# Gate product and residual addition of batches 1 to 5: from VectorE to ScalarE copies and GpSimd products

## The reference

```
xz = rmsnorm(xn) @ in_proj.T;  x_s, z = halves of xz          # 256 channels each
u  = silu(conv4(x_s) + bias)
dt, B, C = u @ x_proj.T;  delta = softplus(dt @ dt_proj.T + b)
h[t] = exp(delta[t] * A) * h[t-1] + delta[t] * u[t] * B[t]    # 16 states per channel
y[t] = sum over states of h[t] * C[t]  +  u[t] * D
mamba = (y * silu(z)) @ out_proj.T + xn
out = x + mamba + (top-2-of-8 experts: silu(xn Wg) * (xn Wu) @ Wd)
```

## Time and profile before

| | |
|---|---|
| median of 3 runs | 635.2 us (634.61 to 636.0) |
| profiled execution, its own time | 637.19 us |
| its span, first to last instruction | 635.4 us |
| VectorE busy | 600.0 us, 94% |
| TensorE busy | 548.8 us, 86% |
| GpSimd busy | 490.9 us, 77% |
| ScalarE busy | 443.7 us, 70% |

### The profile page before, as it was taken

How to read it: one execution, slowest core, us unless ns; L and a number is a source line. 1 busy time by engine, 2 the same in 40 slices (tenths; PEclk the granted TensorE clock), 3 DMA queues, 4 the chain that set the end, 5 groups by cost and what they waited for, 6 DMA issues and landing times.

```text
span 635.4 us, 11450 instructions
## 1 busy us (share of the span) xinstructions
PE 548.8 (86%) x3560; PEld 428.1 (67%) x3560; DVE 600.0 (94%) x867; ACT 443.7 (70%) x891; POOL 490.9 (77%) x466
## 2 busy tenths in 40 slices
PE   5969988898899988989889898998989797878887
PEld 2368666655777777777688677776777465656564
DVE  6966989999999999999999999999999999899997
ACT  1784899128676787667766686776876479969881
POOL 5795039639989799897989879897897877875783
PEclk9867979979999999999999999999999989899999
DMA  7420107924667897777778796678884346332473
GB/s 222 145 84 0 63 10 124 316 101 158 208 230 271 261 304 261 251 254 250 264 263 267 240 300 242 235 262 273 292 269 149 124 162 217 128 118 77 113 146 87
DMA packets 60893, 122.99 MB, mean 194 GB/s; under 512 B 8218, under 2 KB 41378, under 8 KB 53794
## 3 DMA queue, kind: packets, MB, share of 16 engines
q1 hardware_dynamic: 53826, 112.42, 52.0%
q0 software_dynamic: 6288, 9.52, 6.7%
q10 hardware_dynamic: 720, 0.33, 0.2%
HBM read 112.77 MB, written 9.47 MB: 192 GB/s over the span
## 4 chain that ended last, share of the span: by engine, by line
PE 37%; DVE 27%; issue 14%; ACT 12%; POOL 10%; DMA 1%; DVEq 0%; POOLq 0%; ACTq 0%
DVE bank L1091 11%; DVE h_sb L1108 7%; POOL dbu L895 6%; PE bank L1522 6%; PE bank L1375 6%; PE bank L1407 5%; PE bank L1536 4%; PE bank L1530 3%; ACT dbu L530 3%; PE bank L1430 2%; ACT da L502 2%; PE bank L1422 2%; PE bank L1338 2%; POOL xs L882 1%; PE bank L1503 1%
## 5 line engine op out<-in xcount | busy, mean ns | idle before, releaser
L895 POOL TENSOR_TENSOR dbu<-du,xn_all 128x512 f32<-128x512 f32 x172 | 215.4, 1275 | 48.0 <-DVE bank L1091 47.5
L1091 DVE TENSOR_TENSOR_SCAN bank<-bank,dbu 128x512 f32<-128x512 f32 x170 | 207.7, 1224 | 3.4 <-ACT bank L514 3.4
L514 ACT ACTIVATE bank<-delta,a_sb 128x512 f32<-128x512 f32 x170 | 117.0, 690 | 76.9 <-DVE h_sb L1108 76.3
L1108 DVE TENSOR_TENSOR h_sb<-bank,xh_all 128x512 f32<-128x512 f32 x240 | 159.9, 680 | 1.2
L1375 PE MATMUL bank<-id_sb,h_sb 128*128 128x128 f32 x992 | 135.1, 281 | 15.3 <-DVE h_sb L1108 13.7
L1375 PEld LDWEIGHTS bank<-id_sb,h_sb 128*128 128x128 f32 x992 | 115.4, 145 | 27.1 <-DVE h_sb L1108 20.6
L1091 DVE TENSOR_TENSOR_SCAN bank<-da,bank 128x512 f32<-128x512 f32 x82 | 96.8, 1216 | 17.0 <-PE bank L1338 16.9
L1522 PEld LDWEIGHTS bank<-wd_sb,hid 117*128 117x128 f32 (+1 forms) x432 | 55.1, 190 | 55.0 <-DVE hid L1142 31.3
L1522 PE MATMUL bank<-wd_sb,hid 117*128 117x128 f32 (+1 forms) x432 | 64.0, 284 | 25.1 <-ACT xT L667 13.0
L882 POOL DMA_INDIRECT xs<-xn_rows,src x72 | 70.7, 981 | 12.1 <-issue 6.3
L530 ACT ACTIVATE dbu<-du_t,bc_sb 128x256 f32<-128x256 f32 x164 | 69.4, 496 | 4.3 <-DVE bank L1091 2.9
(11 more groups left out here) (192 smaller groups left out, 877.9 us busy)
## 6 DMA issues: line engine op xcount, KB each, us to landing
xh_all<-b_rows SPq DMA_DIRECT2D x30, 1024.0 KB, 6.4
xn_all<-b_rows SPq DMA_DIRECT2D x25, 1024.0 KB
wgu_sb<-in_w_gu SPq DMA_DIRECT2D x72, 352.0 KB, 4.4
wd_sb<-in_w_dn SPq DMA_DIRECT2D x72, 192.0 KB, 5.5
y_slots<-ys SPq DMA_DIRECT2D x72, 64.0 KB
xn_rows<-xn_all SPq DMA_DIRECT2D x2, 1040.0 KB, 11.8
out<-x_sb SPq DMA_DIRECT2D x7, 256.0 KB, 7.5
x_sb<-in_x SPq DMA_DIRECT2D x2, 640.0 KB, 6.3
```

Source lines behind the costliest of these rows:

```text
L514: nc.scalar.activation(bank_of(b, m)[:, :], delta[b % 2][:, hf, :], ACT.Exp, scale=a_sb[:, hf, k:k + 1]).then_inc(s["da_rdy"], 1)
L895: nc.gpsimd.tensor_tensor(dbu[k % 2][:, hf, :], du[b % 2][:, hf, :], b_ring[c % 2][:, k % CH, :], ALU.mult).then_inc(s["dbu_p"], 1)
L1091: nc.vector.tensor_tensor_scan(at, da_of(n)[:, hf, :] if n in IN_SBUF else at, inp, 0.0, ALU.mult, ALU.add).then_inc(s["h_rdy"], 1)
L1108: nc.vector.tensor_tensor(h_sb[k % 2][:, hf, :], bank_of(b, 2 * k + hf)[:, :], row, ALU.mult).then_inc(s["p_rdy"], 1)
```

## The change

In batches 1 to 5, VectorE's two products for z (L1206) and its addition of the projection (L1128) go. For z, ScalarE first copies z from PSUM into `du_t` (an SBUF tile that is free in these batches), makes the tanh as before, and adds one to it; GpSimd multiplies the two, in steps 6 and 9. For the projection, ScalarE copies the bank into `du_t` in step 9, and GpSimd adds it to the sum in step 14. TensorE's waits for the bank now look at ScalarE's reads (`z_th`, `o_ev`). Batches 0, 6 and 7 are as before.

```diff
@@ input_turned(i), ScalarE
+                if i == 1:
+                    act.wait_ge(s["o_rdy"], 5)
@@ early(b, k), ScalarE
+                if b < 6 and k == PROJECT_AT[b] + 2:
+                    projected(b - 1)
@@ z_gate(b, k), ScalarE
                 act.wait_ge(s["z_mm"], 2 * b + i + 1)
+                if 0 < b < 6:
+                    if i == 0:
+                        act.wait_ge(s["z_rdy"], 2 * b)
+                        wait(act, "o_rdy", b - 1)
+                    if b == 1:
+                        act.wait_ge(s["dbuT_a"], S - 1)
+                    nc.scalar.activation(du_t[:, hf, :], z_bank(b)[:, :], ACT.Copy)
                 nc.scalar.activation(zs_sb[:, hf, :], z_bank(b)[:, :], ACT.Tanh, scale=0.5).then_inc(s["z_th"], 1)
+                if 0 < b < 6:
+                    act.wait_ge(s["z_th"], 2 * b + i + 1)
+                    nc.scalar.activation(zs_sb[:, hf, :], zs_sb[:, hf, :], ACT.Identity, bias=sign_sb[:, 0:1]).then_inc(s["z_one"], 1)
+
+            def projected(b):
+                act.wait_ge(s["o_mm"], b + 1)
+                act.wait_ge(s["z_rdy"], 2 * b + 3)
+                nc.scalar.activation(du_t[:, 1, :], FB[0][:, :], ACT.Copy).then_inc(s["o_ev"], 1)
@@ step(b, k), GpSimd
+                if 0 < b < 6:
+                    if k in (6, 9):
+                        gate_z(b, k == 9)
+                    if k == S - 2:
+                        residual(b - 1)
+            def gate_z(b, i):
+                hf = 1 - i
+                pool.wait_ge(s["z_one"], 2 * b - 1 + i)
+                nc.gpsimd.tensor_tensor(zs_sb[:, hf, :], zs_sb[:, hf, :], du_t[:, hf, :], ALU.mult).then_inc(s["z_rdy"], 1)
+            def residual(b):
+                pool.wait_ge(s["o_ev"], b + 1)
+                a_b = acc[:, b * TT:(b + 1) * TT, :]
+                nc.gpsimd.tensor_tensor(a_b, du_t[:, 1, :].rearrange("p (t c) -> p t c", t=TT), a_b, ALU.add).then_inc(s["o_rdy"], 1)
@@ step(b, k), VectorE
-                if k == PROJECT_AT[b] + 1:
-                    store(b - 1, GB if b > 5 else FB[0])
-                if b != 6 and k in z_step(b):
+                if b > 5 and k == PROJECT_AT[b] + 1:
+                    store(b - 1, GB)
+                if b == 7 and k in z_step(b):
@@ conv, z_mm and step of TensorE
-                        pe.wait_ge(s["o_rdy"], c - 2)
+                        pe.wait_ge(s["o_ev"], c - 2)
-                if i:
+                if i and 0 < b < 6:
+                    pe.wait_ge(s["z_th"], 2 * b + 1)
+                elif i:
                     pe.wait_ge(s["z_rdy"], 2 * b + 1)
-                    pe.wait_ge(s["z_rdy"], 2 * b + 2)
+                    pe.wait_ge(s["z_th"], 2 * b + 2)
                     project(b - 1, FB[0])
```

More of the change, by code:

```diff
@@ L199, in build @@
                    br_mm dbu_rdy da_rdy h_rdy p_rdy acc_mm y_out dd_rdy xc_mm x_th x_half u_rdy v_mm
-                   v_out bc_mm bc_rdy z_mm z_rdy sp_exp sp_ln sp_rem sp_w sp_sum z_th delta_rdy du_rdy
+                   v_out bc_mm bc_rdy z_mm z_rdy z_one o_ev sp_exp sp_ln sp_rem sp_w sp_sum z_th delta_rdy du_rdy
                    dut_mm dut_rdy yb_mm g_rdy o_mm o_rdy o_out""".split()
@@ L1204, in z_gate @@
                 i, hf = z_turn(b, k), z_step(b)[k]
+                wait(dve, "z_rdy", 2 * b + i)
                 dve.wait_ge(s["z_th"], 2 * b + i + 1)
```

## The result

| | before | after |
|---|---|---|
| median (20 runs each) | 635.9 us | 632.55 us |
| profiled execution, its own time | 637.19 us | 634.19 us |
| batch period, scan of step 9 in batch 2 to that in batch 3 | 74.88 us | 74.21 us |

The ratio is 0.9949, with a 95% interval of 0.9937 to 0.9960: faster by 3.2 us. The forecast had the direction, but 5.9 us; the change brought little more than half of that. The batch period says it without the scatter of whole executions: 0.67 us shorter, where 1.18 was forecast, and 5 x 0.67 = 3.35. The forecast named a period not 1.2 us shorter as a sign of being wrong, and that is what came. That 632.55 lies in the wide range of 627.6 to 633.0 says nothing for its mechanism.

A forecast was written before the change was run, and what follows sets the result against it. VectorE was taken to bound batches 1 to 5. The sum was -5.9 us for VectorE and 0 each for ScalarE, GpSimd and TensorE: 635.2 - 5.9 = 629.3 us, with a range of 627.6 to 633.0.

The forecast's parts named there:

- a period not 1.2 us shorter: Sign of being wrong: the batch period fails to fall by 1.2 us against before.
- VectorE's loss: Batches 1 to 5: removing two products for z at 0.59 us saves 1.18 us a batch, 5.9 us in five.
- The addition: VectorE's projection addition before the scan of step 9: removal worth nothing, as VectorE waits there for an exponential anyway.
- The forecast's 1.37: VectorE's wait before the scan of step 9, claimed to be 1.37 us instead of 0.68 once the addition is gone.
- GpSimd: Three added operations, 3.8 us a batch, cost nothing: `dbu` of step 16 keeps 0.7 us to spare, 0.4 in batch 1.
- rival 4: GpSimd becomes the bound at `dbu` of step 16; if operations are held while running, 10 us more, 645 us; 5%.
- ScalarE's gain: Added copy and addition of one for z, about 1.23 us, delay exponentials in step 5 within VectorE's margins: costs nothing.
- In step 6 there is no backlog and the margin is larger: ScalarE's second z pair, in step 6, claimed to leave more than the 0.7 and 0.4 us margins of step 5.
- TensorE "still follows VectorE": Steps 4 to 7: TensorE's waits for VectorE, 1.01 and 0.40 us, exceed the 1.18 us shortening, so it costs nothing.
- 4.87 us of ScalarE's own work: Logarithm's chain between the exponentials at 321.55 and 326.42, before the scan of step 9, claimed to be all ScalarE's work.
- Rival 1: All three VectorE removals count, if the logarithm's chain before step 9 shortens by 0.59 us: 626.3 us; 6%.
- Rival 2: GpSimd or ScalarE gives part back, with VectorE waiting at step 16 or in steps 5 and 7: 631.5 us; 19%.

The follow-up runs named there:

- experiments 5 and 6: Against the changed kernel: in 5 VectorE's addition of the projection in step 8 is restored, ratio to before 0.9930; in 6 VectorE's products for z are restored, ratio 0.9989.
- kernel 1: The changed kernel with ScalarE's addition of one moved, in steps 4 and 6, behind the experts' tanh, the copy xT and the weights; ratio to before 0.9887.
- Experiment 9: kernel 1 plus one GpSimd product of no use, 128 x 512, in step 14 of batches 1 to 5; ratio to before 0.9920.
- experiment 7: The changed kernel with ScalarE's output copy of step 8 moved behind the logarithm in the same step; ratio to before 0.9871.

## What of the prediction was right, and which step failed

**VectorE's loss: right.** 0.59 us for a product for z, twice a batch, and the steps follow at 4.36.

**The addition: right.** Worth nothing, since it stood in the wait (experiments 5 and 6). In 6 the wait as the profile counts it grew by 0.59 to 1.27. The forecast's 1.37 is the same wait, counted from where the scan could have started; the profile counts from the end of the instruction ahead, which is 0.1 later.

**GpSimd: right.** 53.83 us against 53.9 between `dbu` of steps 5 and 16, no wait of VectorE. In kernel 1, where VectorE runs as forecast, `dbu` of step 16 in batch 3 starts at 350.65, and 1.28 later its first half is there, 0.75 before the scan at 352.68; the forecast said 0.7. Experiment 9 shows that this room is real and some 0.1 smaller: `dbu` came 1.0 later, and the scan 0.38. The 172 products for `dbu` kept their mean of 1275 ns, and the 15 added ones took 1285 in the median: rival 4's mechanism, that the two engines block each other, did not occur. So far the trace agrees with the Trainium skill's page SBUF — State Buffer, section "Who interferes with whom", by which a VectorE instruction with at most one input in SBUF, outside the 2-port modes, does not contend with GpSimd.

**ScalarE's gain: right in size, wrong in who was asked.** In step 4 copy, tanh and addition took 0.60, 0.61 and 0.72 and pushed the next exponential by 0.48, 0.64 and 0.63 (starts at 302.78, 303.26, 303.90, 304.53), 1.75 in all where 1.83 was worked out. VectorE never waited in steps 5 to 8: the exponential at 306.99 ended 0.55 ahead of its scan at 308.22, where 0.4 was forecast. One remark was wrong: "In step 6 there is no backlog and the margin is larger". ScalarE came into step 6 with a backlog from the wide addition of step 5. There the addition of one starts 2.49 us behind VectorE's scan (312.89 - 310.40), in step 4 it was 2.22, and the next exponential is only 0.58 ahead of its scan (0.84 in step 5). But above all the forecast weighed this lag only against VectorE's scans. The other reader of ScalarE's queue is TensorE, through `xT`, and there the margin was much smaller: in batch 3 before, ScalarE's `xT` of step 6 ended at 315.67, and `hid`, for which TensorE then waited, at 315.96. That is only 0.3 us. Against VectorE's pace the copy came 0.8 us later than before (it had ended 3.57 us behind the scan of step 6 at 312.10, and ended 4.36 behind that at 310.40), and TensorE's product started 0.6 later.

**TensorE "still follows VectorE": the step that failed.** The sum put TensorE at nothing; it cost 2.6 us in five batches. The step was argued from TensorE's waits for VectorE alone: 1.01 + 0.40 is more than 1.18. But the releaser itself changed, from VectorE's `hid` to ScalarE's `xT`. The two waits also stand in different places, one for each product for z, and can't be added up. From the down product of step 7 to that of step 8 TensorE took 5.49 us before (316.01 to 321.50, with the wait of 0.40 in it) and 4.83 after (314.91 to 319.74, with none). That room of 0.66 went nearly whole into the second product's 0.59, and 0.07 was left to make up for a lag of 0.60. And the "4.87 us of ScalarE's own work" from the exponential at 321.55 was not all its own: the output copy started at 322.37, 0.04 behind the end of TensorE's down product (322.33), and some 0.2 later than ScalarE could have. Rival 1 named that link, but only as a gain ("0.2 us at most", and experiment 7 gained 0.25 by cutting it); what a loss there would do was not asked. It is the place through which TensorE's lag of 0.6 came back on VectorE as 0.54 in each of batches 2 to 5 and 0.43 in batch 1, where the wait is 1.70 and not 1.81: 2.6 of the 5.9 us.

**Rival 2** had the nearer sum (630 to 634, say 631.5) and the right engine in part: a margin of ScalarE was used up. That is luck for its number, since the places it named stayed empty: VectorE waited neither in steps 5 or 7 nor for `dbu`.

The logarithm's chain passes a delay that enters it on to VectorE one to one (0.54 in, 0.54 out), since VectorE waits at its end in every batch. The wait grew from 0.68 us to 1.81: 0.59 of that is the addition that no longer fills it and costs nothing, 0.54 is the delay. Experiment 7 shows a way out: let nothing in the chain wait for a third engine.

## What to carry to other kernels

When work is moved to an engine, list all readers of what is queued behind it, not only the engine that bounds the kernel, and give each its own margin from the timeline; here VectorE was left 0.55 us at the tightest, while TensorE had 0.3 and the copy came 0.8 later. If a chain ends in a standing wait of the bounding engine, look for every cross-engine wait inside it: a delay that enters there costs in full, and work that is removed within the wait gains nothing. An addition that nobody needs for two or three steps belongs behind the short copies that someone waits for.

## What was not expected of the hardware

The two table loads of a batch took 1.28 us each, before and after the change, and the logarithm and the exponential started 0.01 to 0.02 behind them. The Trainium skill (ScalarE: Activation LUTs, "What ACT_TABLE_LOAD costs") gives some 2.66 us for a switch, a drain included; the timelines read here show no drain beyond the load's 1.28. By an estimate from that page's figures the chain would be 2.8 us longer a batch with it, and the measurement decides.

GpSimd's product of two separate operands of 128 x 512 took 1275 ns in the mean; the same product with one operand read twice took 1039 to 1060 ns in five records of experiment 9.

```profile
L938 POOL TENSOR_TENSOR du_t<-du_t x5: 1039/1050/1060, 203.6 to 494.4; 128x512 f32<-128x512 f32 x5
```

The part ahead of batch 1 differs between executions by some microseconds: VectorE's gate of batch 0 starts at 139.25 before, 139.56 after and 134.37 in experiment 7, though nothing up to there was changed; over the first 135 us the granted clock of TensorE was 0.89, 0.89 and 0.92 of full speed, and from 40 to 60 us 0.64, 0.64 and 0.85. That the start follows the clock was not tested. The part behind batch 5 differs too: from the gate of batch 5 to the last gate it is 120.0 us before, 120.1 after and 122.5 in experiment 7. Whole executions scatter by some 0.5% either way, while the periods of kernels with the same path agree to 0.02 us (74.20 and 74.21, 73.67 twice, 73.42 twice; one profiled execution each), so the period is the better measure of a change inside a batch.
